# A gated cross-attention block with a mixture of experts: no zero matmuls, one more semaphore, constants and first queries in another order

## What is computed

```python
# x (8, 56, 256), context (8, 1500, 256), 16 heads of 16
q  = _qdq(layernorm(x)) @ _qdq(wq).T + bq        # _qdq: symmetric int8 rounding, scale per row
kv = ctx @ wkv.T + bkv
attn = softmax(einsum('bnhd,bmhd->bhnm', q, k) / 4)
x = x + tanh(g_xattn) * (_qdq(attn @ v) @ _qdq(wp).T + bp)
# router: top 2 of 16 experts by sqrt(softplus(layernorm(x) @ gate_w.T)) + gate_b, at most 128 rows each
y = sum over the two experts of weight * (silu(xe @ W1.T) * (xe @ W3.T)) @ W2.T   + the shared expert
x = x + tanh(g_ffn) * y
```

## Time and profile before

| | us |
|---|---|
| median of 3 runs | 395.81 |
| lowest, highest | 395.68, 406.52 |
| the profiled execution | 396.12 |
| its span, first to last instruction | 394.3 |
| TensorE busy in it | 351.5 (89%) |
| VectorE busy | 294.1 (75%) |
| ScalarE busy | 252.3 (64%) |
| GpSimd busy | 129.4 (33%) |

### The profile page before, as it was taken

The page is one execution under the profiler, slowest core; times in us unless marked ns, Lnnn a source line. Parts: engine busy times, 40 slices in busy tenths (PEclk is TensorE's granted clock), DMA queues, the critical chain, the costliest instruction groups (busy, mean ns, idle before and its releaser), DMA issues.

```text
span 394.3 us, 14146 instructions
## 1 busy us (share of the span) xinstructions
PE 351.5 (89%) x5815; PEld 269.6 (68%) x5815; DVE 294.1 (75%) x680; ACT 252.3 (64%) x428; POOL 129.4 (33%) x120
## 2 busy tenths in 40 slices
PE   7873799989999999999998999998845779999993
PEld 3741478669677768867865967876734577888872
DVE  5732876777876687887676678769895877999983
ACT  3670587767788687688776766676811535766760
POOL 8192332333024132332342300010101054787770
PEclk9999799999999999999999999999975768999999
DMA  7899871664378287177454206652000009645001
GB/s 248 210 222 229 118 203 30 163 154 104 84 127 191 59 144 199 56 119 183 115 83 104 56 28 133 179 145 93 5 2 0 1 1 303 205 123 166 3 2 47
DMA packets 37457, 45.67 MB, mean 116 GB/s; under 512 B 6779, under 2 KB 33467, under 8 KB 37267
## 3 DMA queue, kind: packets, MB, share of 16 engines
q1 hardware_dynamic: 36963, 44.57, 47.1%
q0 software_dynamic: 288, 0.21, 0.3%
q10 hardware_dynamic: 144, 0.00, 0.0%
HBM read 25.08 MB, written 0.47 MB: 65 GB/s over the span
## 4 chain that ended last, share of the span: by engine, by line
PE 74%; DVE 10%; ACT 5%; issue 4%; DMA 2%; POOL 2%; SPq 1%; DVEq 0%; ACTq 0%
PE PS L1118 35%; PE PS L1189 9%; PE PS L1162 9%; PE PS L1200 8%; PE PS L1466 4%; PE PS L1425 4%; DMA gateT<-gate 1%; ACT PT_all L553 1%; PE PS L1449 1%; POOL cT L434 1%; DVE mx L866 1%; SPq L326 1%; PE PS L1176 1%; DMA PT_all<-L_xattn_wkv 1%; PE PS L1382 1%
## 5 line engine op out<-in xcount | busy, mean ns | idle before, releaser
L866 DVE TENSOR_REDUCE mx<-PS 112x1 f32<-112x500 f32 (+1 forms) x128 | 114.1, 932 | 41.7 <-PE PS L1162 41.5
L553 ACT ACTIVATE PT_all<-PS 128x1344 f32<-128x1344 f32 x64 | 82.5, 1290 | 9.7 <-PE PS L1189 9.3
L1118 PE MATMUL PS<-cT,wkvT 128*128 128x500 f16 x288 | 68.8, 378 | 11.4 <-DVE KN L829 7.8
L1118 PE MATMUL PS<-wkvT,cT 128*125 128x256 f16 x576 | 69.9, 273 | 0.0
L1118 PEld LDWEIGHTS PS<-wkvT,cT 128*125 128x125 f16 x576 | 63.6, 136 | 5.5
L434 POOL TENSOR_TENSOR cT<-c_in,cT 128x1000 f16<-128x1000 f32 x21 | 43.7, 2083 | 68.7 <-ACT cT L529 68.7
L1118 PEld LDWEIGHTS PS<-cT,wkvT 128*128 128x128 f16 x288 | 27.6, 98 | 43.2 <-issue 11.0
L1162 PE MATMUL PS<-arena,QC 96*112 96x500 f16 x192 | 51.6, 375 | 3.5 <-POOL QC L463 2.2
L1189 PE MATMUL PS<-QC,arena 98*128 98x112 f16 x768 | 48.6, 213 | 3.4 <-ACT QC L573 3.3
L536 ACT ACTIVATE KN<-PS,col_in 128x500 f16<-128x500 f32 x48 | 32.3, 676 | 28.7 <-PE PS L1118 28.7
L829 DVE SCALAR_TENSOR_TENSOR KN<-PS,col_in,KN 128x500 f16<-128x500 f32 x48 | 35.2, 736 | 19.9 <-ACT KN L536 19.7
(11 more groups left out here) (217 smaller groups left out, 464.3 us busy)
## 6 DMA issues: line engine op xcount, KB each, us to landing
arena<-KN SPq DMA_DIRECT2D x144, 125.0 KB, 4.4
c_in<-ctx SPq DMA_DIRECT2D x24, 500.0 KB, 5.2
cT<-W SPq DMA_DIRECT2D x11, 352.0 KB
c_in<-W SPq DMA_DIRECT2D x6, 352.0 KB
cT<-W SPq DMA_DIRECT2D x11, 176.0 KB
arena<-place_far SPq DMA_DIRECT2D x1, 1568.0 KB, 9.9
c_in<-W SPq DMA_DIRECT2D x6, 176.0 KB
PT_all<-L_xattn_wkv SPq DMA_DIRECT2D x2, 256.0 KB, 3.9
```

Source lines behind the costliest of these rows:

```text
L553: act.activation(PT_all[:, u % 4, :].rearrange("p (c k) -> p c k", c=CH), PS[:, 3:6, 0:4 * TP], ACT.Exp, scale=SCORE).then_inc(s["exp_done ...
L866: dve.tensor_reduce(mx[:, u % 2, k:k + 1], PS[0:TP, k:1 + k * (CH - 1), 0:CW], AX.XY, ALU.max).then_inc(s["red_done"], 1)
L1118: ins = mm(out_, w(a, h), x_(b, h), start=first and k == 0, stop=last and k == len(todo) - 1)
```

## The change

Six edits. The zero matmuls go. The constants of `KS` wait on GpSimd for the quantised query weights, the two fills behind them for the stacked first queries, and the four of the router stand behind the second half of the masked queries; `NCONST` is 22 for TensorE's wait, and VectorE waits for all 26 after attention. `gateT` counts on a semaphore of its own, `gate_loaded`, for which TensorE waits ahead of the router; ScalarE waits for `row_in` alone. On TensorE the turned weights, the second chunk's keys and the first queries' products come ahead of the third value group; ScalarE and VectorE take their parts in that order, and the token scales come ahead of the quantised weights on VectorE. On GpSimd the first low half of the queries and its stacking come ahead of all its other query transfers, and the low halves of context chunks (1, 1) and (1, 2) stand behind the first masked queries.

```diff
-WARM = 14
-NCONST = 26
+NCONST = 22
 # SyncE
-            sp.dma_start(gateT[:], gate).then_inc(s["rows_loaded"], 16)
+            sp.dma_start(gateT[:], gate).then_inc(s["gate_loaded"], 16)
 # GpSimd
+            gp.wait_ge(s["wqq_ready"], 1)
             c.did(gp.memset(KS[QR:QR + 2, 0, 0, :], -1.0))
             c.settle()
             c.did(gp.memset(KS[QR:QR + 1, 0, 0, :], CS))
             c.settle()
...
             gp.dma_start(KS[QR:QR + 2, 0, 1:], KS[QR:QR + 2, 0, 0:1, :].to_broadcast([2, NPAIR - 1, KW])).then_inc(s["ones_spread"], 16)
             gp.dma_start(KS[QR:QR + 2, 1], KS[QR:QR + 2, 0, 0:1, :].to_broadcast([2, NPAIR, KW])).then_inc(s["ones_spread"], 16)
+
+            gp.wait_ge(s["qn_ready"], 1)
+            gp.tensor_tensor(qn[:, :, 1, :], qT[:, :, 0:TP], qn[:, :, 0, :], ALU.subtract).then_inc(s["qn_ready"], 1)
+            gp.wait_ge(s["qn_ready"], 2)
+            gp.dma_start(q16[2 * PW:3 * PW, 0:4, 0:TP], qn[:, 0, 1, :]).then_inc(s["q_stacked0"], 16)
+            for k in (0, 1, 2):
+                gp.dma_start(q16[PW * k:PW * k + PW, 4:8, 0:TP], qn[:, 1, k // 2, :]).then_inc(s["q_stacked1"], 16)
             c.did(gp.memset(KS[0:QR, :, :, M:KW], 0.0))
             c.did(gp.memset(V[:, :, :, :, DH:VW], 1.0))
-            c.did(gp.iota(rank[:], ...))
-            c.did(gp.iota(slot_of[:], ...))
-            c.did(gp.iota(slots[:], ...))
-            c.did(gp.memset(shared_w[:], 0.5 / FS ** 2))
             assert c.n == NCONST
-
-            gp.wait_ge(s["qn_ready"], 1)
-            for k in (0, 1):
-                gp.dma_start(q16[PW * k:PW * k + PW, 4:8, 0:TP], qn[:, 1, 0, :]).then_inc(s["q_stacked1"], 16)
-            gp.tensor_tensor(qn[:, :, 1, :], qT[:, :, 0:TP], qn[:, :, 0, :], ALU.subtract).then_inc(s["qn_ready"], 1)
-            gp.wait_ge(s["qn_ready"], 2)
-            for oh in range(NH):
-                gp.dma_start(q16[2 * PW:3 * PW, 4 * oh:4 * oh + 4, 0:TP], qn[:, oh, 1, :]).then_inc(s[f"q_stacked{oh}"], 16)
             context_lo(1, 0)
-            root(slice(1, 2), 2)
-            context_lo(1, 1)
...
             queries(0, 0)
+            context_lo(1, 1)
+            context_lo(1, 2)
+            root(slice(1, 2), 2)
             gp.wait_ge(s["q_stacked1"], 16 * 3)
             queries(0, 1)
-            context_lo(1, 2)
+            # rank, slot_of, slots, shared_w as above
 # ScalarE
-            keys_hi(0, 1)
             act.wait_ge(s["pe_pre"], 3)
             ap.did(act.activation(wqT[:], ...))
+            keys_hi(0, 1)
+            query_hi(0, qn)
             evacuate_values(0, 2)
-            query_hi(0, qn)
...
-            act.wait_ge(s["rows_loaded"], 32)
+            act.wait_ge(s["rows_loaded"], 16)
 # VectorE
+            dve.wait_ge(s["consts"], EARLY)
+            spread_scales([0])
             dve.wait_ge(s["wq_loaded"], 16 * NH)
             quantise(wq_in, NH, swq_am, swq, wq16).then_inc(s["wqq_ready"], 1)
-            dve.wait_ge(s["consts"], EARLY)
-            spread_scales([0])
             context_lo(0, 1)
             keys_lo(0, 0)
             context_lo(0, 2)
-            keys_lo(0, 1)
             dve.wait_ge(s["act_pre"], 5)
             dve.wait_ge(s["pe_pre"], 4)
             query_product(...)
+            keys_lo(0, 1)
...
             w13_lo(0)
+            dve.wait_ge(s["rows_loaded"], 16)
+            dve.wait_ge(s["consts"], NCONST + 4)
 # TensorE
-            pe.wait_ge(s["consts"], 1)
-            for k in range(WARM):
-                mm(PS[0:TP, 3, :], zero16[:, 0:TP], zero16[:], start=True, stop=True)
...
             turn_scales(0, 1, 0)
-            project_keys(0, 1)
             # the four turns of the query weights
-            project_values(0, 2)
+            project_keys(0, 1)
             pe.wait_ge(s["act_pre"], 6)
             project_queries(0, 2, 0)
+            project_values(0, 2)
             project_values(0, 3)
...
+            pe.wait_ge(s["gate_loaded"], 16)
             for k, part in enumerate(groups):   # router
```

More of the change, by code:

```diff
@@ L254, in bank16 @@
             return PS[:, b, :].bitcast(F16)
-        names = """consts var_ready rstd_ready sp_ready x_loaded x_rest wq_loaded wp_loaded wk_loaded wv_loaded cols_loaded rows_loaded xq_ready x0_ready xr_ready wqq_ready wpq_ready
+        names = """consts var_ready rstd_ready sp_ready x_loaded x_rest wq_loaded wp_loaded wk_loaded wv_loaded cols_loaded rows_loaded gate_loaded xq_ready x0_ready xr_ready wqq_ready wpq_ready
             sx_diag sp_diag gate_ready pe_pre act_pre dve_pre qn_ready qb_done q_stacked0 q_stacked1 q_hi0 q_late qp_read dve_step
@@ L425, in _, with context_lo @@
             gp.wait_ge(s["rstd_ready"], 1)
+            def context_lo(n, c):
+                need(gp, "th_done", n * CH + c + 1)
+                gp.tensor_tensor(cT[:, n % 2, 1, :, c * CW:(c + 1) * CW], c_in[:, :, c * CW:(c + 1) * CW],
+                                 cT[:, n % 2, 0, :, c * CW:(c + 1) * CW], ALU.subtract).then_inc(s["tl_done"], 1)
+            gp.wait_ge(s["wqq_ready"], 1)
             c.did(gp.memset(KS[QR:QR + 2, 0, 0, :], -1.0))
@@ L469, in _ @@
             queries(0, 0)
+            context_lo(1, 1)
+            context_lo(1, 2)
+            root(slice(1, 2), 2)
             gp.wait_ge(s["q_stacked1"], 16 * 3)
             queries(0, 1)
-            context_lo(1, 2)
+            c.did(gp.iota(rank[:], [[0, TT], [-1, E]], base=E, channel_multiplier=0, allow_small_or_imprecise_dtypes=True))
+            c.did(gp.iota(slot_of[:], [[0, 1]], base=0, channel_multiplier=1, allow_small_or_imprecise_dtypes=True))
+            c.did(gp.iota(slots[:], [[1, CAP]], base=0, channel_multiplier=0, allow_small_or_imprecise_dtypes=True))
+            c.did(gp.memset(shared_w[:], 0.5 / FS ** 2))
             gp.wait_ge(s["xr_ready"], 1)
```

7 lines of the change are left out of this document (removed).

## The result

| | before | after |
|---|---|---|
| median, us | 399.19 (20 runs) | 395.03 (20 runs) |
| lowest, highest | 395.68, 406.67 | 389.37, 402.73 |
| the profiled execution | 396.12 | 391.25 |
| its span | 394.3 | 389.4 |

The ratio is 0.9868, 95% interval 0.9831 to 0.9906: a gain, and within 2%. The kernel before is itself 3.4 us slower in these runs than in the three shown ahead; scaled to those, after stands at 0.9868 x 395.81 = 390.6 us, still 5.0 us above the forecast. The profiled pair differs by 4.87 us, where my sum had 10.25.

A forecast was written before the change was run, and what follows sets the result against it. TensorE was taken to bound the kernel, except a 7.95 us wait behind `gateT`. Scores 0 earlier (-1.7), gap (-7.95), pace (-1.35) and VectorE's lag (+0.75) gave -10.25: 385.9 us profiled, 385.6 predicted, range 383.0 to 389.6.

The forecast's parts named there:

- the first key group: TensorE's first real keys, without zero matmuls: start at 8.2 to 8.4 us, taking 2.7 us.
- the six key groups: TensorE's key groups ahead of scores 0: through at 27.55 us, with 2.5 us for the clock.
- The row of the pace: Zero matmuls at 0.426 us per 512 columns, 1.2 GHz: removing them costs 2.5 us of TensorE.
- the clock column: Granted clock 1.00 at 3 to 4 us: by it alone, removing the zero matmuls loses nothing.
- the gap: TensorE idle from 33.08 to 41.03 us behind ScalarE's wait for `gateT`; the new semaphore removes it: -7.95 us.
- (3): Constants later on GpSimd: TensorE's start moves from 8.90 to 8.25 us; later constants run beside VectorE at no cost.
- (4): Queries earlier: rounded at 19.0 us, lower half landing at 25.4 after 5.2, masked by 26.4 to 26.9 against 29.0.
- Rival B: Query transfers queue behind the constants' broadcasts: masked queries end at 30.0 us, 2.7 us back, 388.3 us; chance 0.12.
- The clock after the start: Half pace for 5.0 us of TensorE's first work, costing 2.5 us, bounds 1.75 and 2.8.
- Rival D: The clock stays down until batch 1 is under way: +8.5 us, 404.3 us; chance 0.03.
- VectorE's lag: Slot 2's scores wait for slot 1's maxima, behind tile 1's scale chain: +0.75 us, bounds 0 to 1.5.
- The stretch keeps its 236 us: TensorE from 46 to 282 us, busy 230.2 of 236.0, shifts unchanged; otherwise the prediction is wrong.

The follow-up runs named there:

- e6: The kernel after with 8 zero matmuls ahead of slot 0 and 6 in slot 1; median 394.34 us, ratio 0.987 to before.
- e7: The kernel after with tile 1's scale chain on VectorE moved behind slot 1's maxima; median 391.94 us, ratio 0.981 to before.
- e4: The kernel after without GpSimd's wait ahead of the constants, so they run early again; median 392.49 us, ratio 0.984 to before.
- e10: e8 with e7's edit, tile 1's scale chain behind slot 1's maxima; median 389.76 us, ratio 0.976 to before.
- e13: e10 with batch 1's stacked key copies held back until slot 3's turned scores; median 392.81 us, ratio 0.978 to before.
- e8: e4 with the loads of batch b+3's context behind the stacked copies of batch b+1; median 390.23 us, ratio 0.975 to before.
- e9: e8 with most of batch 1's key copies replaced by GpSimd fills, its results left wrong; median 393.12 us, ratio 0.985 to before.

## Why the prediction was wrong

**Right.** The tanh without idle for a transfer; the first key group at half pace (2.66 us), though at 8.62 and not at 8.25; the normalised and rounded tokens in 0.41 and 0.29 us once the fills had gone; rounded queries at 19.1 (predicted 19.0); the six key groups through at 27.6 (27.55). The row of the pace was the one to believe, not the clock column. What I called likeliest, that the gap goes, went.

Three steps failed in the profiled pair, and a fourth where they are mended. The differences add up to that pair:

| | us |
|---|---|
| predicted | -10.25 |
| scores 0 at 29.55 instead of 27.6 | +1.95 |
| clock and order from scores 0 to slot 1's scores (4.86 us; before 3.18) | +1.68 |
| slot 1's to slot 2's scores, 4.78 us instead of the 4.37 of the sum | +0.4 |
| slot 2's to slot 3's scores, 6.03 us instead of 3.86 | +2.17 |
| slot 3 to slot 63 | +0.06 |
| behind the slots | -0.88 |
| profiled pair | -4.87 |

**(3) and (4), constants and queries.** I costed the issues of the constants on GpSimd, at nothing, and never SyncE's queue, whose copies are issued while those transfers run. One of them took 2.67 us there. The queries' high half was issued at 21.8 and landed 5.83 us after 22.46; the lower half, on which I had worked out the masked queries, was not the last. Rival B had the direction (queries late because of the constants) and another mechanism. With early constants the second high half is issued 2 us sooner, which is the size of this term. The other mis-sized term is its landing: 5.2 us was my figure for a query transfer, and 5.6 to 10.6 were measured, so this 1.95 us would be another number in another execution.

**The clock after the start.** My sum let it rise once and stay. It fell again about a wait of 1.93 us ahead of scores 0, and at 40 us behind waits of 1.47, 0.44 and 0.35: 3.1 us in all by e6. Rival D counted only on its never rising. Around the wait of 2.17 us at the same place in the kernel before, it had not fallen. In the sixteen profiles it fell there in eight of the nine with a wait of 1.93 us or more, and in none of the six with 1.25 or less. (e6, the sixteenth, had zeros in the wait.)

**The overlooked wait.** I let VectorE's lag hold slot 2's scores, 0.75 us. It holds the turn of slot 0's maxima first: the turn writes the PSUM bank from which slot 1's scores are reduced, and waits for slot 1's first reduction, which stands behind tile 1's scale chain. That is 1.47 us of wait, and its fall of the clock. In the kernel before the chain ran beside the third key group, which came at half pace, and the turn behind it didn't wait. e7 moves the chain and gets 1.16 us between those two rows.

**The stretch keeps its 236 us.** This was the assumption I had named as the one to fail. It is no part of the profiled pair's miss, where slots 3 to 63 came out even (+0.06): before has holes of its own there, 1.08 us at 85.95 and 1.43 at 206.99, after has others. But where the head is mended, the lead of 9 to 10 us at slot 0 doesn't reach the end: 2.6 of 9.9 us are left in e4, 4.0 of 9.6 in e10, 6.8 of 9.4 in e13. The head is then early, its stacked copies and the context loads come without the pause that the 7.95 us of waiting had given the transfer engines, and TensorE's own instructions come late. The stretch was never bounded by matmuls alone; of the 5.8 us idle in its "busy 230.2 of 236.0", which I didn't look at, 2.5 are those two holes. It took early constants and e8's order of loads to come near what I had forecast for the change alone: 0.975 of 395.81 is 386.1 us.

A part of the miss is none of the change: 3.4 us lie between the medians of before in the two sets of runs. One slip bears on nothing: by its own bounds of the clock and of VectorE's lag the forecast spans 384.1 to 386.7 us, not 384.5 to 387.

## What to carry to other kernels

A wait that is taken away also was a pause for whatever ran beside it: before counting it as gained, ask what the transfer engines and the instruction supply did in it. Look for "issue" holes inside runs of equal matmuls, and for the share of the transfer engines there; try big loads behind the copies that are needed first, and not in one block with them (e8 against e4: the hole went from 4.09 to 1.41 us, the times aren't told apart). And when one queue's work is moved beside another's, price both queues' issues, and list what each wait in the stretch releases, in program order, before trusting that "it is the engine's own time".

## What was not expected of the hardware

- TensorE stood still for 0.5 to 4.70 us inside runs of equal matmuls, and resumed 2.4 to 3.6 us after the start of a 16 KB instruction transfer. None of the 107 such transfers that met transfer engines at a share under 0.3 had a hole behind it, 48 of the 339 at 0.6 or more had. Behind the two longest holes (4.09 and 4.70 us) the granted clock fell too.
- SyncE took 3.7 to 4.0 us to issue three stacked copies while GpSimd's two spreading transfers were under way, and 1.84 to 1.89 without.
- The granted clock fell about a wait of 1.93 us of TensorE (after) and not about one of 2.17 (before); fourteen zero matmuls ahead of the first work held the full pace through the first key group in one kernel's profile of five.
- A fill of `arena` by GpSimd stretched a VectorE operation from 0.35 to 4.20 us (e9). The Trainium skill ("SBUF — State Buffer", "Terms") has the two engines share a pair of ports that the loser waits for; the trace agrees, with the operation's end at 42.2 and the fill's at 42.1. In small it stands in the earlier trace rows: the normalisation took 0.98 us beside a fill and 0.41 in after without one, while the subtraction at 7.57 took no longer beside one than the other without.
